# First block's x turned into banks by features, an identity turned in front of it, weights' low parts moved between the first evictions, gate sums in four parts

## The chip, the cores and the metric
One NeuronCore of a Trainium2 chip. The metric is the device time of the whole program in microseconds, the median of several runs.

## The reference
x is 16 x 1024 tokens of 512 features, taken here as 16384 rows. What is computed, in short:

```python
x = x + linear_attn(layernorm(x))   # 16 heads of 32; phi = elu + 1 on q and k, causal sums of k v^T and k
x = x + moe(layernorm(x))           # softmax gate over 8 experts, top 2, capacity 1.25*N/E
# an expert over its capacity (counts > cap) is dropped whole: valid = (counts <= cap)[a_e]
```

Projections are `x @ W.T + b`; the attention output divides the numerator `q . sum(k v^T)` by `q . sum(k) + 1e-6`.

## The kernel before, in words
The 16384 tokens are 32 blocks of 512 (`BT`), each of 4 tiles of 128 (`TPB`). A block passes three stages: **turn** (x normalised, features on the partitions, split into a high part `xt_hi` and a low part `xt_lo` of reduced-precision floats), **proj** (K, Q and V), and **attn** (scores, numerators, output product, residual). In the steady state one step (`Step`) runs attn of one block, proj of the next and turn of the one after it, interleaved by tile `c` = 0 to 3. The program starts with a step that only turns block 0, then a step that projects block 0 and turns block 1 (`attn` is false in both); each engine's `body(st)` is its own list in program order, and `run` calls it. Nothing reorders these lists: an instruction that waits holds all behind it on its engine.

Every product is three products, hi*hi, hi*lo, lo*hi, over 4 groups of features `k`: 12 matmuls of 512 columns make one K or Q chunk (`project`, L660), two times 12 of 260 columns a V chunk (`two_halves`, L678). Below, K0 is chunk 0 of K, and so on; the order on TensorE is K0 Q0 K1 Q1 K2 Q2 K3 Q3 V0 V1 V2 V3. Their results go to a ring of six PSUM banks: K0, K1 to bank 0, Q0, Q1 to bank 1, K2, K3 to bank 5, Q2, Q3 to bank 0. After a K or Q chunk ScalarE does a Relu and an Exp from the bank (`relu_exp`, L848 and L850) and VectorE `phi` (L944) reads the bank and frees it; for K, `key_sums` adds a scan (L954) and a copy (L956). V chunks are evicted by `values` (L963, L965).

The start: SyncE loads x, then the weights (256 KB pieces by 128 columns for K and Q, whole for Wo, Wv, Wo^T). VectorE takes moments (L1016), GpSimd the reciprocal deviations, VectorE normalises (L996). TensorE turns tile c into bank c by four transposes (`turn_first`, L648), ScalarE takes `xt_hi` (L854), VectorE `xt_lo` (L1002). Each weight piece is split the same way: `split_high` on ScalarE (L327), `split_low` on VectorE (L332). Before, ScalarE splits all eight K and Q pieces, and VectorE all eight low parts, in front of the first eviction (`split_first`, `set_first`):

```python
def set_first():
    split_low(dve, "wq_t", 0)
    set_biases(dve)
    for name, g in SPLITS[2:2 * KD]:
        split_low(dve, name, g)
```

Wv is split in one piece in front of K2's eviction. `sum_gates` (L377) multiplies Wo's stage with the gate's 8 columns, 4 products for each of 4 groups: groups 0 and 1 behind Q2, 2 and 3 behind Q3:

```python
if c == 1 and not attn:
    sum_gates(pe, (0, 1))
```

In the second step VectorE also takes `divide` (L992, q times the reciprocal denominator) and the low parts of block 1 (`split_x_low`, L1008) in front of V3's eviction. Block 1's K0 goes to V3's bank 0, so it waits for that eviction.

## Time and profile before

| | |
|---|---|
| median of 3 runs | 1926.53 us (1926.5 to 1927.26) |
| profiled execution, device time | 1929.05 us |
| its span | 1927.3 us |
| granted TensorE clock, mean | 0.996 |
| TensorE busy | 98% |
| VectorE, ScalarE, GpSimd busy | 82%, 34%, 46% |
| DMA | 218 MB, mean 113 GB/s |

Read it so: the span is the profiled execution from its first to its last instruction; the device time has 1.75 us more around it. The profiled execution is 2.5 us above the median of the runs that were only timed.

### The profile page before, as it was taken

The numbers are of one execution on the slowest core, as the hardware profiler recorded it, in microseconds if no ns is written. First come the engines' busy times: TensorE is split into PE (matmuls) and PEld (weight loads), VectorE is DVE, ScalarE is ACT, GpSimd is POOL, SyncE is SP. The second block draws the span as 40 slices with busy tenths as digits, with TensorE's granted clock in tenths as the row PEclk, the third lists the DMA queues.
The fourth block names the chain that finished last, engine by engine and source line by source line (L and its number), as shares of the span: only waits on it lengthen the run. The fifth ranks groups of instructions, "written<-read, shape, count | busy, mean of one in ns | idle before, by whom it ended". The sixth has DMA issues, their size and how long they took to land. (4 is left out here: it accounts for less than half of the span.)

```text
span 1927.3 us, 60211 instructions
## 1 busy us (share of the span) xinstructions
PE 1894.4 (98%) x25412; PEld 1662.2 (86%) x25412; DVE 1580.7 (82%) x3379; ACT 663.7 (34%) x1297; POOL 890.8 (46%) x981
## 2 busy tenths in 40 slices
PE   7999999999999999999999999999999999999996
PEld 6888888888888888888888888888888888888885
DVE  6878777888879887878878987878788897878787
ACT  4333333333333333333333333333333333333331
POOL 3345553455453555534554444555445544355522
PEclk9999999999999999999999999999999999999998
DMA  6343234333233332333433344323433324343222
GB/s 208 100 133 111 87 108 132 117 119 111 91 123 120 124 122 76 123 123 111 128 101 103 112 124 131 111 90 108 130 116 122 106 89 127 120 124 122 73 72 79
DMA packets 171199, 218.00 MB, mean 113 GB/s; under 512 B 24368, under 2 KB 85808, under 8 KB 170928
## 3 DMA queue, kind: packets, MB, share of 16 engines
q1 hardware_dynamic: 170928, 214.13, 35.3%
q8 instruction: 201, 3.29, 0.7%
q14 instruction: 70, 0.57, 0.1%
HBM read 151.02 MB, written 63.04 MB: 111 GB/s over the span
## 5 line engine op out<-in xcount | busy, mean ns | idle before, releaser
L1286 POOL TENSOR_TENSOR k_sum<-k_sum,q_raw 128x512 f32<-128x512 f32 x128 | 165.3, 1291 | 553.0 <-DVE q_raw L944 553.0
L848 ACT ACTIVATE e_tmp<-ring,bias_n 128x512 f32<-128x512 f32 x256 | 176.2, 688 | 508.9 <-PE ring L660 506.5
L933 DVE TENSOR_TENSOR s_mask<-ring,causal 128x512 f32<-128x512 f32 x512 | 314.6, 675 | 0.0
L678 PE MATMUL ring<-wv_hi,xt_hi 128*128 128x260 f32 x1024 | 298.9, 292 | 0.0
L678 PE MATMUL ring<-wv_hi,xt_lo 128*128 128x260 f32 x1024 | 289.2, 282 | 0.0
L678 PE MATMUL ring<-wv_lo,xt_hi 128*128 128x260 f32 x1024 | 289.2, 282 | 0.0
L678 PE MATMUL ring<-wo_hi,o_hi 128*128 128x260 f32 x1024 | 287.0, 281 | 2.0 <-ACT o_hi L898 1.9
L678 PE MATMUL ring<-wo_hi,o_lo 128*128 128x260 f32 x1024 | 286.7, 284 | 1.1 <-DVE o_lo L1185 1.1
L678 PE MATMUL ring<-wo_lo,o_hi 128*128 128x260 f32 x1024 | 287.7, 282 | 0.0
L898 ACT ACTIVATE o_hi<-num_ps 128x512 fp32r<-128x512 f32 x128 | 76.4, 597 | 467.9 <-PE num_ps L758 467.9
L660 PE MATMUL ring<-xt_hi,wk_hi 128*128 128x512 f32 x512 | 208.6, 407 | 3.3 <-DVE xt_lo L1002 1.7
L1281 POOL TENSOR_TENSOR x_in<-x_in,x_rows 128x512 f32<-128x512 f32 x124 | 204.2, 1647 | 9.7
L1279 POOL TENSOR_TENSOR x_in<-x_in,x_rows 128x512 f32<-128x512 f32 x124 | 198.1, 1598 | 18.3 <-DMA x_rows<-moments_rows 18.3
L678 PEld LDWEIGHTS ring<-wv_hi,xt_hi 128*128 128x128 f32 x1024 | 192.7, 188 | 12.1 <-issue 0.4
L660 PE MATMUL ring<-xt_hi,wk_lo 128*128 128x512 f32 x512 | 201.6, 394 | 0.0
L660 PE MATMUL ring<-xt_lo,wk_hi 128*128 128x512 f32 x512 | 200.6, 392 | 0.0
L660 PE MATMUL ring<-xt_hi,wq_lo 128*128 128x512 f32 x512 | 199.6, 390 | 0.0
L660 PE MATMUL ring<-xt_hi,wq_hi 128*128 128x512 f32 x512 | 199.2, 389 | 0.0
L660 PE MATMUL ring<-xt_lo,wq_hi 128*128 128x512 f32 x512 | 199.2, 389 | 0.0
L678 PEld LDWEIGHTS ring<-wo_hi,o_hi 128*128 128x128 f32 x1024 | 192.8, 188 | 5.3 <-ACT o_hi L898 2.4
L944 DVE SCALAR_TENSOR_TENSOR k_t<-ring,bias,e_tmp 128x512 f32<-128x512 f32 x128 | 95.9, 749 | 121.3 <-ACT e_tmp L850 116.7
L678 PEld LDWEIGHTS ring<-wo_lo,o_hi 128*128 128x128 f32 x1024 | 192.1, 188 | 2.9
(142 smaller groups left out, 4055.2 us busy)
## 6 DMA issues: line engine op xcount, KB each, us to landing
x_tok<-in_x SPq DMA_DIRECT2D x128, 256.0 KB, 3.9
res<-in_x SPq DMA_DIRECT2D x128, 256.0 KB, 2.7
out<-res SPq DMA_DIRECT2D x128, 256.0 KB, 2.1
x_in<-in_x_t SPq DMA_DIRECT2D x124, 256.0 KB, 4.6
keys_turned<-k_turned SPq DMA_DIRECT2D x112, 256.0 KB, 2.0
k_tok<-keys_turned SPq DMA_DIRECT2D x448, 64.0 KB, 2.0
x_rows<-moments_rows SPq DMA_DIRECT2D x31, 512.0 KB, 3.6
k_t<-in_wk_t SPq DMA_DIRECT2D x4, 256.0 KB, 4.5
```

Of the source, the lines that this page charges most:

```text
L660: mm = pe.matmul(bank, w[a][:, k, g * P:(g + 1) * P], xt[b][:, k, :], start=n == 0, stop=n == 3 * KD - 1)
L678: mm = pe.matmul(bank[:, 0:HW], rows[a](k), w[b][:, k, h, :], start=n == 0, stop=n == 3 * KD - 1)
L848: act.activation(e_tmp[:, m], bank, ACT.Relu, bias=bias_n[:, m, g:g + 1], scale=-1.0).then_inc(phi_relu.handle, 1)
L898: act.activation(o_wide[0], num, ACT.Copy).then_inc(o_hi.handle, 1)
L933: dve.tensor_tensor(s_mask[:, j], ring[:, st.bank(u)].rearrange("p (g t) -> p g t", g=KD), repeat(causal, KD), ALU.mult).then_inc(free[st. ...
L944: dve.scalar_tensor_tensor(out, bank, bias[:, m, g:g + 1], e_tmp[:, m], ALU.add, ALU.max).then_inc(free[st.bank(u)].handle, 1)
L1279: pool.tensor_tensor(x, x, repeat(x_rows[:, :, c, 0], KD), ALU.subtract).then_inc(x_centred.handle, 1)
L1281: pool.tensor_tensor(x, x, repeat(x_rows[:, :, c, 1], KD), ALU.mult).then_inc(x_normed.handle, 1)
L1286: pool.tensor_tensor(k_sum[:, g], k_sum[:, g], q_raw[:, g], ALU.mult).then_inc(prod.handle, 1)
```

## The change
Parts, in the order of the program:

1. Wk's stage is now `s_mask`, Wq's the second half of `q_div`, so that the stages outlive the first evictions into `k_t` and `q_raw`. Pieces 0 and 1 of both are loaded ahead of the small columns (biases, gate) instead of piece 0 alone.
2. `keep_busy`: 24 transposes of the identity into bank 0, once the second tile's moments are taken.
3. `turn_first` writes the transpose of feature group k to bank 2+k at the tile's columns, so a bank holds one feature group of all four tiles, and is full with the last tile. ScalarE and VectorE split bank by bank; `project_first` does K0 in the order hi*hi, hi*lo(weights), lo*hi for each k, waiting for each k's own parts.
4. ScalarE's and VectorE's splits of the other pieces stand between the first evictions; Wv is split in two halves. The scans follow later. VectorE takes block 1's moments behind Q0's eviction.
5. The gate sums are four parts, behind K2, Q2, K3 and Q3.
6. In the second step VectorE takes the low parts of block 1's tiles 0 and 1 ahead of V2's eviction, instead of behind `divide`; GpSimd's `rstds` come before its first product.

```diff
+TURN_BANKS = [2 + k for k in range(D // P)]
+WARMING = 24
...
-                    load_weights(sp, LOADS[:2])
+                    load_weights(sp, LOADS[:4])
                     load_columns(sp)
-                    load_weights(sp, LOADS[2:-3])
+                    load_weights(sp, LOADS[4:-3])
...
+        def keep_busy():
+
+            pe.wait_ge(x_stat.handle, x_stat.at(2))
+            for _ in range(WARMING):
+                pe.transpose(ring[:, 0, 0:P], ident, ident)
+
         def turn_first(c):
 
-            pe.wait_ge(free[c].handle, free[c].at(0))
             pe.wait_ge(x_normed.handle, x_normed.at(c + 1))
-            for k in range(KD):
-                mm = pe.transpose(ring[:, c, k * P:(k + 1) * P], x_tok[:, c, k * P:(k + 1) * P], ident)
-            mm.then_inc(full[c].handle, 1)
+            for k, b in enumerate(TURN_BANKS):
+                if c == 0:
+                    pe.wait_ge(free[b].handle, free[b].at(0))
+                mm = pe.transpose(ring[:, b, c * P:(c + 1) * P], x_tok[:, c, k * P:(k + 1) * P], ident)
+                if c == TPB - 1:
+                    mm.then_inc(full[b].handle, 1)
+
+        def project_first():
+
+            u = ("K", 0)
+            bank = ring[:, BANK[u]]
+            pe.wait_ge(free[BANK[u]].handle, free[BANK[u]].at(0))
+            pe.wait_ge(ready["wk_t"].handle, 1)
+            for k, b in enumerate(TURN_BANKS):
+                pe.wait_ge(xt_hi.handle, xt_hi.at(k + 1))
+                for a in range(2):
+                    pe.matmul(bank, w_k[a][:, k, 0:P], xt[0][:, k, :], start=k == 0 and a == 0, stop=False)
+                pe.wait_ge(free[b].handle, free[b].at(1))
+                mm = pe.matmul(bank, w_k[0][:, k, 0:P], xt[1][:, k, :], start=False, stop=k == KD - 1)
+            mm.then_inc(full[BANK[u]].handle, 1)
...
-                if c == 1 and not attn:
-                    sum_gates(pe, (0, 1))
...
+                if c == 1 and not attn:
+                    for place in range(2, 4):
+                        chunks(st, c, place)
+                        sum_gates(pe, (place,))
...
+        def first_chunks(st):
+
+            split_high(act, "wk_t", 1)
+            split_high(act, "wq_t", 1)
             act.wait_ge(bias_set.handle, BIASES)
+            relu_exp(st, "K", 0)
+            split_high(act, "wk_t", 2)
+            split_high(act, "wq_t", 2)
+            relu_exp(st, "Q", 0)
+            split_high(act, "wk_t", 3)
+            split_high(act, "wq_t", 3)
+            relu_exp(st, "K", 1)
+            split_high(act, "wv_t", 0)
+            relu_exp(st, "Q", 1)
+            split_high(act, "wv_t", 1)
...
+                if c == 2 and not attn:
+                    split_x_low(st, 0)
+                    split_x_low(st, 1)
```

Where the instructions stand. **ScalarE, evictions of K1 to K2**: `v_tok` is Wv's stage, `e_tmp` what Relu and Exp write. Before:

```order
L848 ACTIVATE e_tmp<-ring,bias_n 128x512 [waits ring_free0,ring_full0]
L850 ACTIVATE e_tmp<-e_tmp 128x512 [waits phi_relu]
L848 ACTIVATE e_tmp<-ring,bias_n 128x512 [waits ring_free1,ring_full1]
L850 ACTIVATE e_tmp<-e_tmp 128x512 [waits phi_relu]
L327 ACTIVATE wv_hi<-v_tok 128x8x256 [waits load_wv_t]
L848 ACTIVATE e_tmp<-ring,bias_n 128x512 [waits ring_free0,ring_full5]
L850 ACTIVATE e_tmp<-e_tmp 128x512 [waits phi_relu]
```

Now:

```order
L877 ACTIVATE e_tmp<-ring,bias_n 128x512 [waits ring_free0,ring_full0]
L879 ACTIVATE e_tmp<-e_tmp 128x512 [waits phi_relu]
L330 ACTIVATE wv_hi<-v_tok 128x4x256 [waits load_wv_t]
L877 ACTIVATE e_tmp<-ring,bias_n 128x512 [waits ring_free1,ring_full1]
L879 ACTIVATE e_tmp<-e_tmp 128x512 [waits phi_relu]
L330 ACTIVATE wv_hi<-v_tok 128x4x256 [waits load_wv_t]
L877 ACTIVATE e_tmp<-ring,bias_n 128x512 [waits ring_free0,ring_full5]
L879 ACTIVATE e_tmp<-e_tmp 128x512 [waits phi_relu]
```

The split of Wv, which waits for its load, stood behind Q1's Relu and Exp; now its first half stands ahead of them.

**VectorE, evictions of K1 to K2**: `k_t` and `q_raw` are what phi writes, `k_sum` the scan. Before:

```order
L944 SCALAR_TENSOR_TENSOR k_t<-ring,bias,e_tmp 128x512 [waits phi_exp,ring_full0]
L954 SCALAR_TENSOR_TENSOR k_sum<-k_t 128x512 [waits ring_free0]
L956 COPY k_carry<-k_sum 128x1 [waits k_scan]
L944 SCALAR_TENSOR_TENSOR q_raw<-ring,bias,e_tmp 128x512 [waits phi_exp,ring_full1]
L332 TENSOR_TENSOR wv_lo<-v_tok,wv_hi 128x8x256 [waits high_split]
L338 CAST wv_hi<-gates 128x8x4
L340 TENSOR_TENSOR wv_lo<-gates,wv_hi 128x8x4 [waits gate_split]
L944 SCALAR_TENSOR_TENSOR k_t<-ring,bias,e_tmp 128x512 [waits phi_exp,ring_full5]
L954 SCALAR_TENSOR_TENSOR k_sum<-k_t 128x512 [waits ring_free5]
```

Now:

```order
L984 SCALAR_TENSOR_TENSOR k_t<-ring,bias,e_tmp 128x512 [waits phi_exp,ring_full0]
L335 TENSOR_TENSOR wk_lo<-s_mask,wk_hi 128x4x128 [waits high_split]
L984 SCALAR_TENSOR_TENSOR q_raw<-ring,bias,e_tmp 128x512 [waits phi_exp,ring_full1]
L335 TENSOR_TENSOR wq_lo<-q_div,wq_hi 128x4x128 [waits high_split]
L994 SCALAR_TENSOR_TENSOR k_sum<-k_t 128x512 [waits ring_free0]
L996 COPY k_carry<-k_sum 128x1 [waits k_scan]
L984 SCALAR_TENSOR_TENSOR k_t<-ring,bias,e_tmp 128x512 [waits phi_exp,ring_full5]
```

Wv's low part left the place in front of K2's phi; Wk's and Wq's last low parts and K0's scan came there.

**TensorE, the start**: `ring` is the PSUM ring. Before:

```order
L648 MATMUL ring<-ident,x_tok 128x128 [waits x_normed,ring_free0,ident_set]
L648 MATMUL ring<-ident,x_tok 128x128 x3
L648 MATMUL ring<-ident,x_tok 128x128 [waits x_normed,ring_free1]
L648 MATMUL ring<-ident,x_tok 128x128 x3
L648 MATMUL ring<-ident,x_tok 128x128 [waits x_normed,ring_free2]
L648 MATMUL ring<-ident,x_tok 128x128 x3
L648 MATMUL ring<-ident,x_tok 128x128 [waits x_normed,ring_free3]
L648 MATMUL ring<-ident,x_tok 128x128 x3
L660 MATMUL ring<-xt_hi,wk_hi 128x512 [waits ring_free3,ready_wk_t,ring_free2,ring_free0,ring_free1]
L660 MATMUL ring<-xt_lo,wk_hi 128x512
```

Now:

```order
L649 MATMUL ring<-ident 128x128 [waits x_stat,ident_set]
L649 MATMUL ring<-ident 128x128 x23
L657 MATMUL ring<-ident,x_tok 128x128 [waits ring_free2,x_normed]
L657 MATMUL ring<-ident,x_tok 128x128 [waits ring_free3]
L657 MATMUL ring<-ident,x_tok 128x128 [waits ring_free4]
L657 MATMUL ring<-ident,x_tok 128x128 [waits ring_free5]
L657 MATMUL ring<-ident,x_tok 128x128 [waits x_normed]
L657 MATMUL ring<-ident,x_tok 128x128 x3
L657 MATMUL ring<-ident,x_tok 128x128 [waits x_normed]
L657 MATMUL ring<-ident,x_tok 128x128 x3
L657 MATMUL ring<-ident,x_tok 128x128 [waits x_normed]
L657 MATMUL ring<-ident,x_tok 128x128 x3
```

The 24 transposes of the identity are new and first; the turning is 16 transposes in both.

## Rows read from the trace of the kernel before

**Rows 1.** Page, busy time of TensorE over the span.
```profile
PE 1894.4 (98%) x25412; PEld 1662.2 (86%) x25412; DVE 1580.7 (82%) x3379; ACT 663.7 (34%) x1297; POOL 890.8 (46%) x981
```

**Rows 2.** Waits of PE over the whole span: us in total, times, longest us.
```profile
PE ring L660 <- DVE gate_x L965: 1.3, 1, 1.3
PE ring L660 <- DVE k_t L944: 0.3, 1, 0.3
```

**Rows 3.** Timeline, PE, first block: start us, us, engine, line, op, [idle before].
```profile
9.79 3.65 PE L648 MATMUL ring<-ident,x_tok 128*128 128x128 f32 x16 [9.79 <-DVE x_tok L996]
...
15.15 0.76 PE L660 MATMUL ring<-xt_hi,wk_hi 128*128 128x512 f32 x1 [1.72 <-DVE xt_lo L1002]
15.71 0.63 PE L660 MATMUL ring<-xt_lo,wk_hi 128*128 128x512 f32 x1
16.14 0.63 PE L660 MATMUL ring<-xt_hi,wk_lo 128*128 128x512 f32 x1
...
19.50 0.40 PE L660 MATMUL ring<-xt_hi,wk_lo 128*128 128x512 f32 x1
```

**Rows 4.** Timeline, DVE and ACT, beside the turning.
```profile
4.53 0.66 DVE L1016 BATCH_NORM_STATS2 stats<-x_tok 128x6 f32<-128x512 f32 x1
...
9.10 1.92 DVE L996 TENSOR_SCALAR x_tok<-x_tok,mv 128x512 f32<-128x512 f32 x4 [0.68 <-POOL mv L1261]
...
13.47 0.60 ACT L854 ACTIVATE xt_hi<-ring 128x512 fp32r<-128x512 f32 x1 [0.26 <-PE ring L648]
...
14.10 0.69 DVE L1002 TENSOR_TENSOR xt_lo<-ring,xt_hi 128x512 fp32r<-128x512 f32 x1 [0.16 <-ACT xt_hi L854]
```

**Rows 5.** Timeline, PE, around the gate sums.
```profile
33.38 1.84 PE L377 MATMUL num_ps<-gates,q_div 128*128 128x8 f32 x16
35.52 0.47 PE L660 MATMUL ring<-xt_hi,wk_hi 128*128 128x512 f32 x1 [0.29 <-DVE k_t L944]
...
39.93 0.39 PE L660 MATMUL ring<-xt_hi,wq_hi 128*128 128x512 f32 x1
...
42.65 1.85 PE L377 MATMUL num_ps<-gates,q_div 128*128 128x8 f32 x16
44.35 0.37 PE L678 MATMUL ring<-wv_hi,xt_hi 128*128 128x260 f32 x1
```

**Rows 6.** Windows, PE: window, us, busy (instructions), PEclk, DMA share, GB/s.
```profile
36.00:37.00 1.00, 1.00 (x4) 0.50 0.49 186
```

**Rows 7.** Timeline, ACT and DVE, around the split of V's weights.
```profile
29.40 1.90 ACT L327 ACTIVATE wv_hi<-v_tok 128x2048 fp32r<-128x2048 f32 x1
31.21 0.67 ACT L848 ACTIVATE e_tmp<-ring,bias_n 128x512 f32<-128x512 f32 x1
31.91 0.63 ACT L850 ACTIVATE e_tmp<-e_tmp 128x512 f32<-128x512 f32 x1
...
31.34 3.05 DVE L332 TENSOR_TENSOR wv_lo<-v_tok,wv_hi 128x2048 fp32r<-128x2048 f32 x1 [0.53 <-ACT wv_hi L327]
...
34.62 0.74 DVE L944 SCALAR_TENSOR_TENSOR k_t<-ring,bias,e_tmp 128x512 f32<-128x512 f32 x1
35.40 1.22 DVE L954 TENSOR_TENSOR_SCAN k_sum<-k_t 128x512 f32<-128x512 f32 x1
```

**Rows 8.** DMA issues (us to landing), SP's timeline, and one window's load.
```profile
v_tok<-in_wv_t SPq DMA_DIRECT2D x1, 1024.0 KB, 11.0
...
18.10 0.51 SPq L311 DMA_DIRECT2D v_tok<-in_wv_t  x1
...
7.50:9.50 2.00, 0.00 (x0) 0.00 (x0) 1.17 (x4) 0.63 (x1) 1.68 (x6) 1.00 0.68 56
```

**Rows 9.** Timeline, DVE, ACT and PE, end of the first projections.
```profile
58.11 2.49 DVE L1008 TENSOR_TENSOR xt_lo<-x_in,xt_hi 128x512 fp32r<-128x512 f32 x4
...
58.79 0.63 ACT L861 ACTIVATE xt_hi<-x_in 128x512 fp32r<-128x512 f32 x1 [2.88 <-PE ring L678]
...
61.15 0.47 PE L660 MATMUL ring<-xt_hi,wk_hi 128*128 128x512 f32 x1 [1.28 <-DVE gate_x L965]
```

More of the change, by code:

```diff
@@ L456, in give @@
             eng.sem_inc(s.handle, s.credit)
-    base_m1 = [int(k < TPB) for k in range(NBANK)]
+    base_m1 = [int(k in TURN_BANKS) for k in range(NBANK)]
     base_0 = [a + b for a, b in zip(base_m1, per_bank(("proj", "turn")))]
@@ L519, in load_x @@
             if a == 1:
-                for c in range(TPB):
-                    sp.wait_ge(full[c].handle, full[c].at(1))
+                for k in TURN_BANKS:
+                    sp.wait_ge(full[k].handle, full[k].at(1))
             if a > 1:
@@ L777, in body @@
             if not attn and not proj:
+                keep_busy()
                 for c in range(TPB):
@@ L782, in body @@
                 last = c == TPB - 1
-                if proj:
-                    if c == 0 and not attn:
-                        for k in range(TPB):
-                            pe.wait_ge(free[k].handle, free[k].at(1))
-                    elif c == 0:
+                if c == 0 and not attn:
+                    project_first()
+                    chunks(st, c, 1)
+                elif c == 1 and not attn:
+                    for place in range(2):
+                        chunks(st, c, place)
+                        sum_gates(pe, (place,))
+                elif proj:
+                    if c == 0:
                         pe.wait_ge(xt_lo.handle, xt_lo.at(TPB * (st.off + 1)))
@@ L814, in body @@
                     scores(st, st.off + 1, 0)
-                if c == 1 and not attn:
-                    sum_gates(pe, (2, 3))
                 if attn:
@@ L878, in body @@
             if not attn and not proj:
-                for c in range(TPB):
-                    split_first_high(c)
+                for k, b in enumerate(TURN_BANKS):
+                    split_first_high(k, b)
                 return
@@ L889, in body @@
                     split_x_high(st, 1)
-                if c == 1 and not attn:
-                    split_high(act, "wv_t")
-                if proj:
+                if c == 0 and not attn:
+                    first_chunks(st)
+                elif proj:
                     chunks(st, c, 0, 1)
@@ L1150, in body @@
                 split_low(dve, "wk_t", 0)
-                for c in range(TPB):
-                    split_first_low(c)
+                set_biases(dve)
+                for k, b in enumerate(TURN_BANKS):
+                    split_first_low(k, b)
                 return
@@ L1155, in body @@
                 last = c == TPB - 1
-                if c == 1 and not attn:
-                    split_low(dve, "wv_t")
-                    split_gates(dve, "wv_t", gw.rearrange("p k (h e) -> p k h e", h=2), 0)
                 if c < 2 and attn and proj:
@@ L1166, in body @@
                     residual_moments(st, 2)
-                if proj:
+                if c < 2 and not attn:
+                    (first_chunks, next_chunks)[c](st)
+                elif proj:
                     chunks(st, c, 0, 1)
@@ L1170, in body @@
                     divide(st)
-                if c == 0 and not attn:
-                    moments(st, range(TPB))
-                if last and turns:
+                if last and attn and turns:
                     split_x_low(st, 0)
@@ L1212, in body @@
                     split_x_low(st, 3)
-                if proj and (attn or c != 2):
+                if proj and (attn or last):
                     chunks(st, c, 2, 3)
@@ L1236, in body, with first_chunks, next_chunks @@
                 last_logits(st)
-        def set_first():
+        def first_chunks(st):
             split_low(dve, "wq_t", 0)
-            set_biases(dve)
-            for name, g in SPLITS[2:2 * KD]:
-                split_low(dve, name, g)
+            split_low(dve, "wk_t", 1)
+            phi(st, "K", 0)
+            split_low(dve, "wq_t", 1)
+            split_low(dve, "wk_t", 2)
+            phi(st, "Q", 0)
+            split_low(dve, "wq_t", 2)
+            moments(st, range(TPB))
+            phi(st, "K", 1)
+            split_low(dve, "wk_t", 3)
+            phi(st, "Q", 1)
+            split_low(dve, "wq_t", 3)
+            key_sums(st, 0)
+        def next_chunks(st):
+            phi(st, "K", 2)
+            key_sums(st, 1)
+            phi(st, "Q", 2)
+            split_low(dve, "wv_t", 0)
+            key_sums(st, 2)
+            split_low(dve, "wv_t", 1)
+            split_gates(dve, "wv_t", gw.rearrange("p k (h e) -> p k h e", h=2), 0)
+            phi(st, "K", 3)
+            key_sums(st, 3)
+            phi(st, "Q", 3)
             set_from_constants(dve)
@@ L1246, in _ @@
         give(dve, *free, o_lo, x1_stat)
-        run(dve, body, set_first)
+        run(dve, body)
         choose(5, range(CHOOSE_STEPS))
@@ L1358, in body @@
                     pool.tensor_tensor(res[:, c % 2], res[:, c % 2], bo_row, ALU.add).then_inc(res_bias.handle, 1)
+                if c == 0 and not attn:
+                    rstds(st)
                 if proj:
                     chunks(st, c, 0, 1)
-                if c == (1 if attn else 0) and turns:
+                if c == 1 and attn and turns:
                     rstds(st)
```

44 lines of the change are left out of this document (21 added, 23 removed).

## The prediction
> **What bounds the kernel now.** I read the page's busy times first: TensorE is busy 98% of the span [rows 1]. So only its gaps and slow stretches are worth looking for, and its list of waits puts those of the projections at 1.3 and 0.3 us, once each [rows 2]; both lie in the first 62 us, the only stretch that the change rewrites. Behind it TensorE is nearly never idle, so what it gains or loses up to block 1's K0 (start 61.15 us) I carry to the end in full.
>
> In the timeline of that stretch three things cost TensorE time. First, a late and slow start: the turning begins at 9.79, the first real matmul at 15.15 after 1.72 us of idle, and these matmuls take 0.63 us each, 0.43 us apart, where later ones take 0.40 [rows 3]. Twelve matmuls of K0 thus last to 19.73 (19.50 plus one pace of 0.23). The pace at the full level is Q3's: 39.93 to 42.65 for 12, 2.72 us or 0.227 each [rows 5]. Second, the gate sums: 16 instructions of 8 columns from 33.38, then 0.29 us idle for VectorE's phi of K2, and K3 starts at 35.52. It needs 4.41 us, until 39.93, instead of 2.72 [rows 5]; the granted clock is 0.50 in that stretch, the lower level of 1.2 GHz [rows 6]. TensorE had done only the narrow gate products and nothing for 2.14 us before the clock fell. The second run of gate sums, 1.70 us, did not bring it down [rows 5]. Third, 1.28 us idle before block 1's K0, for V3's eviction, which stands on VectorE behind the low parts of block 1 [rows 9].
>
> **The change, part by part.**
>
> *Warming and turning.* The transposes of the identity may start when the second moments are done, 5.19 us [rows 4], say 5.3. Sixteen transposes took 3.65 us, some 0.21 each [rows 3]; 24 take 5.1 us, to 10.4, which is 0.6 later than the turning starts now. That is the cost if the clock stays low. At the high level they would take half, and the x tiles (from 9.10, four in 1.92 us [rows 4]) would set the pace instead. Bounds: turning later by 0.6, or its end earlier by 1.6 to 2. I take the first, from the row nearest to it: the present 16 transposes run from 9.79 to 13.44, and 1.7 us later the matmuls still run at the slow pace [rows 3]. So the last four transposes end at 13.4, 13.6, 13.8 and 14.05. The page "TensorE: Matmul & The Clock Gate" of the Trainium skill, section on PE-mode transpose, says that transpose-mode work does not count as busy for the clock gate; by that rule the 24 transposes are pure cost, and the trace does not contradict it.
>
> *K0 piece by piece.* Now K0 waits for the whole chain turn, high part (0.60), low part (0.69), and the hand-over of 0.36 (14.79 to 15.15) [rows 3, 4]. After, its first matmul needs only the high part of bank 2: 13.4 + 0.6 + 0.36 = 14.35. The parts of the next banks follow every 0.6 us (VectorE's and ScalarE's pace in such a row), while the three matmuls of one bank need 1.28, so none of them waits. If the clock rises at the same time as now (about 18.9), 10.7 of the 12 run slow, and K0 is over at 19.2: 0.5 earlier. If it rises 3.8 us after the first matmul, as now, at 18.8.
>
> *Splits between evictions.* On their own they fit: the K and Q pieces that chunk n+1 needs are split while chunk n runs. From K0's end the chunks need 4 x 2.72 for Q0, K1, Q1, K2, then 0.85 of gates, 2.72 for Q2, 0.85: K3 could start at 19.2 + 15.35 = 34.6. But ScalarE's queue now holds the first half of Wv's split ahead of Q1's Relu. Wv's load is issued at 18.10 and lands 11.0 later, at 29.1 [rows 8], where ScalarE would be there at 19.2 + 7 = 26.2. Loading K and Q pieces 1 ahead of the columns fills part of a stretch in which the queues move 56 GB/s [rows 8]; the columns then push pieces 2 and 3 back by 1.1 us, so I take Wv 0.4 earlier, 28.7 (bounds 27.5 and 29.6). From the landing: half split 0.95, Relu and Exp 1.35, phi of Q1 0.75, Wq's last low part 0.65, K0's scan and copy 1.35, phi of K2 0.75, hand-over 0.15: 6.0 us [rows 4, 7]. K3 starts at 34.7, by this chain or by TensorE's own, which meet here. Term: 35.52 - 34.7 = **0.8**. It cannot go below nothing unless Wv lands past 29.5.
>
> *Gate sums in four.* The work is the same, 2 x 1.70 or 4 x 0.85. Each low stretch is 0.85 us between two chunks of 2.72, less than half of the 1.70 that left the clock up [rows 5]. K3 at full pace: 4.41 - 2.72 = **1.7**. Bounds: nothing (if the clock falls for another reason) and 1.7.
>
> *V0 to V2.* VectorE is then busy without a pause from Q1's phi to V0's evictions: phis, scans, two halves of Wv's low part (3.05 in one piece [rows 7]). Counted instruction by instruction it has V0's first bank free in time for V1; this hides within about 0.2 us, and if Wv's low halves take more than 1.5 each it appears one for one. I put it at nothing.
>
> *Low parts before V2's eviction.* VectorE spends 2.49 us on four low parts between divide and V3's eviction [rows 9]. Two go away from there. But the last of them needs its high part, and ScalarE waits for V3's end on TensorE with that (58.79, 0.63 long [rows 9]). So V3's eviction moves from 60.52 to about 60.05 in these times, not by 1.25: **0.45**.
>
> Sum: 0.8 + 1.7 + 0.45 = 2.95, rounded to 2.9. The profiled execution would go from 1929.05 to 1926.1 (span 1924.4), and the median, which lies 2.5 below the profiled time, from 1926.53 to **1923.6**. A measurement of this kernel can tell about 0.2%, 3.9 us, from no change: the forecast is a gain that lies within that.
>
> **The rivals.**
>
> *A. The clock's fall at the gate sums is the profiled run's own.* The profiled execution is 2.5 us above the median, and 1.7 of it may be this. For: the second gate stretch left the clock up, so the fall is not certain each time. Against: the timed runs lie within 0.8 us, less than 1.7. Then the gain is 0.8 + 0.45 = 1.25: 1925.3. Chance 0.2.
>
> *B. The warming works.* The identity's transposes raise the clock; K0 runs at the full pace right behind the pieces, ends near 15.5 instead of 19.7. But Wv still holds Q1's Relu until 28.7 + 0.95, so K3 still starts at 34.7; TensorE, done with its work at 15.5 + 15.35 = 30.9, idles 3.8 us, and its clock falls there as after the 2.14 us of now. The early 3.7 us are lost, and the 1.7 perhaps too: 1923.6 to 1925.3. Chance 0.12. For: ScalarE's wait for Wv depends only on its order and the load. Against: the present transposes raised nothing.
>
> *C. Wv comes early and the start is quick.* With the load at 27.3 or before and the warm start, K3 starts at 33.3: 2.2 + 1.7 + 0.45 = 4.35, 1922.2. Chance 0.13, since only both together give it.
>
> *D. Wv comes late, and the new wait costs more than the old.* The last bank now fills at 14.05, so block 1's loads, ahead of Wv in the queue, are issued 0.6 later, and the queue could run dry or the column loads hold the rest up. Up to a landing at 31 the change still breaks even (K3 at 37, no slow stretch). Landing at 32.1, K3 starts at 38.1, TensorE idles 3.5 and K3 is slow again: V0 at 38.1 + 7.15 + 1.7 = 46.95 against 44.35 [rows 5], less 0.45, is 2.1 us slower: 1928.6. Against: 11.0 us to landing shows a deep backlog, which 0.6 us don't empty. Chance 0.05, and 0.03 for over 3.9 us.
>
> **How the numbers follow.** The forecast has 0.5, A 0.2, B 0.12, C 0.13, D 0.05. Faster by over 0.2% means below 1922.7: C and the low tail of the forecast, 0.18. Slower by over 0.2%, 0.03. Within, 0.79. The range runs from 1922.0 (C) to 1926.0 (A with Wv late by 0.7), and leaves out D and the tails, some 0.2.
>
> **What would show it.** In the profile after: first real matmul near 14.35 and at the slow spacing of 0.43; the 24 transposes 0.21 apart, not 0.11; ScalarE idle about 2.4 us at Wv's high part, on the load; K3 at 34.7, 2.7 us long, clock 1.00 from the rise near 19 on; block 1's K0 near 58.2 instead of 61.15, with some 0.8 us of idle before it. A warm K0 makes B or C true; K3 late with a full clock lays it on Wv. If block 1's K0 gains 3 and the time doesn't, the carrying in full is wrong.

## The result, and the profile after

| | before | after |
|---|---|---|
| median | 1926.6 us (1925.62 to 1927.26, 6 runs) | 1935.3 us (1932.71 to 1935.64, 6 runs) |
| ratio | | 1.0038, 95% interval 1.0028 to 1.0049 |
| profiled execution, its span | 1929.05, 1927.3 us | 1932.71, 1930.9 us |
| block 1's K0 starts | 61.15 us [rows 9] | 67.76 us |
| last instruction of VectorE starts | 1921.45 us | 1928.14 us |

The change makes the kernel slower by 0.38%: 8.7 us between the medians, 7.3 by the ratio, where I had forecast 2.9 us less. In the profiles the work ends 6.7 us later (last instruction of VectorE), but the span grows by 3.6 only, because the stretch behind that instruction is 3 us shorter (last section). TensorE is as busy as before, and its list of waits names three new ones. Page and waits of PE, kernel after:

```profile
PE 1900.1 (98%) x25436; PEld 1666.5 (86%) x25436; DVE 1594.3 (83%) x3380; ACT 663.6 (34%) x1298; POOL 894.2 (46%) x981
```
```profile
PE ring L684 <- DVE k_t L984: 3.8, 1, 3.8
PE ring L702 <- DVE gate_x L1005: 2.6, 1, 2.6
...
PE ring L702 <- DVE wv_lo L343: 1.7, 1, 1.7
```

All of it is in the first 68 us. Timeline of PE, kernel after (start us, us, engine, line, op, [idle before]), first block and start:

```profile
5.21 4.39 PE L649 MATMUL ring<-ident 128*128 128x128 f32 x24 [5.21 <-DVE stats L1055]
9.69 2.02 PE L657 MATMUL ring<-ident,x_tok 128*128 128x128 f32 x16
12.16 0.47 PE L670 MATMUL ring<-xt_hi,wk_hi 128*128 128x512 f32 x1 [0.45 <-ACT xt_hi L883]
...
15.21 0.48 PE L684 MATMUL ring<-xt_hi,wq_hi 128*128 128x512 f32 x1
```

The start is far better than forecast. The 24 transposes are 0.18 apart on average: three in each quarter of a microsecond up to 8.5, four or five from there on. The 16 of the turning take 2.02 us [rows 3: 3.65], the first real matmul comes at 12.16, and these matmuls run 0.23 apart from the fourth on (the first three, which wait for their pieces, 0.31 to 0.34). Q0 starts at 15.21; before, at 19.73. Four and a half microseconds are won here. Then, from the gate sums to block 1's K0:

```profile
26.84 1.03 PE L380 MATMUL num_ps<-gates,q_div 128*128 128x8 f32 x8 [0.44 <-DMA q_div<-in_wo]
...
30.56 0.95 PE L380 MATMUL num_ps<-gates,q_div 128*128 128x8 f32 x8
35.34 0.47 PE L684 MATMUL ring<-xt_hi,wk_hi 128*128 128x512 f32 x1 [3.83 <-DVE k_t L984]
...
43.41 0.95 PE L380 MATMUL num_ps<-gates,q_div 128*128 128x8 f32 x8
46.03 0.58 PE L702 MATMUL ring<-wv_hi,xt_hi 128*128 128x260 f32 x1 [1.67 <-DVE wv_lo L343]
...
61.50 0.39 PE L702 MATMUL ring<-wv_hi,xt_hi 128*128 128x260 f32 x1 [2.61 <-DVE gate_x L1005]
...
67.76 0.47 PE L684 MATMUL ring<-xt_hi,wk_hi 128*128 128x512 f32 x1 [0.51 <-DVE gate_x L1005]
```

TensorE idles 3.83 us before K3, which starts at 35.34, as late as before [rows 5: 35.52]; 1.67 us before V0; 2.61 us before V3. And the granted clock falls to its lower level, 1.2 GHz, at each of the three; below, the stretch of matmuls at that level is called slow. Windows of PE (window, us, busy, PEclk, DMA share, GB/s):

```profile
36.00:37.00 1.00, 1.00 (x4) 0.50 0.55 207
46.00:47.00 1.00, 0.97 (x4) 0.51 0.00 0
63.00:64.00 1.00, 1.00 (x7) 0.54 0.00 0
```

K3 is thus as slow as before (4.42 us, to 39.76; before 4.41), V0 takes 4.49 and V3 4.25, where a V chunk of 24 matmuls at the full clock takes 2.96. (The PEclk of this view helps at these three places only. Before a program's first rise it reads 1.00 as well, in the kernel before too, where K0's matmuls are 0.43 apart; there the spacing of the instructions tells the level.) That adds up: V0's wait 1.67 and slow stretch 1.53, V3's wait 2.61 and slow stretch 1.29, the third and fourth gate sums with Q3 between them 0.2 more than Q3 and one double one, less 0.18 at K3's start and 0.77 at K0's wait (1.28 to 0.51): 6.3 of the 6.6 us by which block 1's K0 is late; the scores (L755) behind V3, still slow, take 0.33 more. From there on the shift stays between 6.6 and 7.8 us; the last instruction of VectorE is 6.7 late.

The terms of this sum depend on one another. In e3 below, whose lists behind the start are the same, V0 waits 1.85 us and then runs at the full clock; it ends 1.46 earlier, and still V3 starts at 61.50, now behind 3.17 us of idle. What V0's slow stretch costs, V3's wait gives back.

What TensorE waits for at K3 comes through ScalarE. Timeline of ACT, kernel after:

```profile
29.43 1.06 ACT L330 ACTIVATE wv_hi<-v_tok 128x1024 fp32r<-128x1024 f32 x1 [7.11 <-DMA v_tok<-in_wv_t]
30.40 0.67 ACT L877 ACTIVATE e_tmp<-ring,bias_n 128x512 f32<-128x512 f32 x1
```

Wv lands at 29.4 (issued 18.27, 11.1 us to landing), ScalarE has been idle for 7.11 us, and Q1's Relu stands behind the first half. Q1, finished on TensorE at 23.5, is evicted at 31.8 by VectorE.

What it waits for at V0 and V3 is VectorE, and there the durations changed. V0 waits for its own weights, the low part of the gate columns (L343), and V3 for the eviction of V2. Timelines of DVE and POOL, kernel after:

```profile
33.10 1.22 DVE L994 TENSOR_TENSOR_SCAN k_sum<-k_t 128x512 f32<-128x512 f32 x1
...
35.11 1.84 DVE L994 TENSOR_TENSOR_SCAN k_sum<-k_t 128x512 f32<-128x512 f32 x1
...
37.73 1.85 DVE L335 TENSOR_TENSOR wv_lo<-v_tok,wv_hi 128x1024 fp32r<-128x1024 f32 x1
39.50 2.58 DVE L994 TENSOR_TENSOR_SCAN k_sum<-k_t 128x512 f32<-128x512 f32 x1
...
42.19 2.40 DVE L335 TENSOR_TENSOR wv_lo<-v_tok,wv_hi 128x1024 fp32r<-128x1024 f32 x1
44.51 1.24 DVE L341 CAST wv_hi<-gates 128x32 fp32r<-128x32 f32 x1
...
56.02 1.03 DVE L1239 SCALAR_TENSOR_TENSOR rden<-rden_high,lo_rows,den 128x256 fp32r<-128x256 f32 x1
56.97 4.07 DVE L1047 TENSOR_TENSOR xt_lo<-x_in,xt_hi 128x512 fp32r<-128x512 f32 x2
```
```profile
37.22 1.28 POOL L1349 TENSOR_TENSOR k_sum<-k_sum,q_raw 128x512 f32<-128x512 f32 x1 [1.35 <-DVE k_carry L996]
38.45 2.55 POOL L1342 TENSOR_TENSOR x_in<-x_in,x_rows 128x512 f32<-128x512 f32 x1
41.08 2.42 POOL L1344 TENSOR_TENSOR x_in<-x_in,x_rows 128x512 f32<-128x512 f32 x1
43.47 2.24 POOL L1349 TENSOR_TENSOR k_sum<-k_sum,q_raw 128x512 f32<-128x512 f32 x1
...
56.71 1.86 POOL L1342 TENSOR_TENSOR x_in<-x_in,x_rows 128x512 f32<-128x512 f32 x1
58.65 1.85 POOL L1344 TENSOR_TENSOR x_in<-x_in,x_rows 128x512 f32<-128x512 f32 x1
```

The kernel before, for comparison (DVE and POOL; L332 at 63.71 is Wo's low part, as large as Wv's):

```profile
34.31 0.17 DVE L338 CAST wv_hi<-gates 128x32 fp32r<-128x32 f32 x1
...
63.71 2.28 DVE L332 TENSOR_TENSOR wo_lo<-k_t,wo_hi 128x2048 fp32r<-128x2048 f32 x1
```
```profile
36.69 1.53 POOL L1279 TENSOR_TENSOR x_in<-x_in,x_rows 128x512 f32<-128x512 f32 x1 [4.45 <-DMA x_rows<-moments_rows]
38.30 1.54 POOL L1281 TENSOR_TENSOR x_in<-x_in,x_rows 128x512 f32<-128x512 f32 x1
```

The same scan takes 1.22 us at 33.10 and 2.58 at 39.50; half of Wv's low part 1.85 and 2.40, where I had put at most 1.5; the conversion of the 32 gate columns (L341) 1.24 instead of the 0.17 that it took before; two low parts of x 4.07, where four took 2.49 [rows 9]. Compare the ends: the scan from 39.50 is over at 42.08, and its own 1.2 us would begin at 40.86, near the end of GpSimd's product of 38.45 (41.00). The half from 42.19 is over at 44.59, 1.1 us behind the end of the product of 41.08 (43.50). The conversion ends at 45.75, with the product of 43.47 (45.71). GpSimd's products are stretched as well, 2.55 and 2.42 against 1.53 and 1.54 us for the same two in the kernel before. The two engines take turns. Between K2's phi and V0 five instructions of VectorE are longer by this (0.62, 0.63, 1.36, 1.18 and 1.07), together 4.9 us; without them V0's weights would be ready at about 41.1, three microseconds before TensorE comes to V0 (an estimate from these rows). In the kernel before they hardly met up to block 1's K0; the 3.05 of Wv's low part [rows 7], which runs beside a GpSimd product of 30.95 to 32.24, is the one large trace of it, and Wo's, of the same size, takes 2.28.

The Trainium skill has this, in "SBUF — State Buffer", "Who interferes with whom": a VectorE instruction with two inputs in SBUF contends with a GpSimd instruction that reads SBUF, and the ports that they share are an exclusive lock. The trace agrees: 2.58 instead of 1.22 for a scan.

### The profile page after: what moved, and what is told of

Read it like the earlier page. It is cut to its first block and busy times, and to the rows that moved or that the text cites. A ratio compares the mean times of both kernels' runs of the same rounds, so it can differ in the third digit from the quotient of the medians.

```text
span 1930.9 us, 60259 instructions
## 1 busy us (share of the span) xinstructions
PE 1900.1 (98%) x25436; PEld 1666.5 (86%) x25436; DVE 1594.3 (83%) x3380; ACT 663.6 (34%) x1298; POOL 894.2 (46%) x981
## 5 line engine op out<-in xcount | busy, mean ns | idle before, releaser
L702 PEld LDWEIGHTS ring<-wv_hi,xt_lo 128*128 128x128 f32 x1024 | 194.5, 190 | 0.0
```

The lines of the kernel that those rows point to most:

```text
L702: mm = pe.matmul(bank[:, 0:HW], rows[a](k), w[b][:, k, h, :], start=n == 0, stop=n == 3 * KD - 1)
```

## The experiments

Three theories. **T1**: Wv's wait ahead of Q1's Relu idles TensorE and lets the clock fall; everything that is late there then falls together on VectorE. **T2**: the low parts ahead of V2's eviction hold V3. **T3**: VectorE's instructions are late because GpSimd's products block them. Rivals: the identity, the turning or the gate sums in four cost the time. Ratios are to the kernel before on the same chip.

**e1: Wv's halves behind K2's and Q2's Relu and Exp on ScalarE** (VectorE's order stays).

```diff
-                elif proj:
+                elif proj and (attn or c != 1):
                     chunks(st, c, 0, 1)
...
             relu_exp(st, "K", 1)
-            split_high(act, "wv_t", 0)
             relu_exp(st, "Q", 1)
+            relu_exp(st, "K", 2)
+            split_high(act, "wv_t", 0)
+            relu_exp(st, "Q", 2)
             split_high(act, "wv_t", 1)
```

> Only ScalarE's order changes: the two halves of Wv's high part stand behind K2's and Q2's Relu and Exp instead of in front of Q1's and K2's. Theory 1 (ScalarE holds Q1's Relu until Wv lands near 29.4, and TensorE waits 3.8 us at K3 for that): the wait at K3 goes, K3 starts at 31 to 32 instead of 35.34 and at the full clock (2.7 us instead of 4.4); VectorE's Wv low halves are done before GpSimd begins with block 1 near 37, so V0 starts at 37.8 to 40 instead of 46.03. Block 1's K0 comes 5 us or more earlier than 67.76, and the time falls by 5 to 9. Rival (VectorE is short of time in this stretch whatever ScalarE does): K3 starts earlier, but V0 stays within 2 us of 46 and the time within 2 us.

Measured: 1928.98 us (1926.84 to 1934.56, 10 runs), ratio 1.0007 [0.9997, 1.0017]. K3 starts at 32.47 and runs at the full clock, V0 at 39.81 without a wait, block 1's K0 at 63.27 instead of 67.76. V3 still waits 3.12 us and is slow. Timelines of PE and DVE, e1:

```profile
55.76 0.58 PE L702 MATMUL ring<-wv_hi,xt_hi 128*128 128x260 f32 x1 [3.12 <-DVE gate_x L1007]
...
63.27 0.47 PE L684 MATMUL ring<-xt_hi,wk_hi 128*128 128x512 f32 x1 [0.64 <-DVE gate_x L1007]
```
```profile
51.28 4.02 DVE L1049 TENSOR_TENSOR xt_lo<-x_in,xt_hi 128x512 fp32r<-128x512 f32 x2
```

T1's share is 4.5 us of the start of block 1's K0; T2's is left.

**e2: the low parts of tiles 0 and 1 back behind `divide`.**

```diff
-                if c == 2 and not attn:
-                    split_x_low(st, 0)
-                    split_x_low(st, 1)
...
-                if last and attn and turns:
+                if last and turns:
                     split_x_low(st, 0)
                     split_x_low(st, 1)
```

> Only VectorE's low parts of block 1's tiles 0 and 1 go back behind divide. Theory 1 (these two, 4.07 us for 2, wait behind GpSimd's normalisation of the last tile and hold V2's eviction, so V3 waits 2.6 us and runs at the low clock): V3's wait of 2.61 us goes, V3 takes 3.1 instead of 4.3, block 1's K0 comes 3 to 3.5 us earlier than 67.76, K3 stays at 35.3. Rival (the two just take long in this place for a reason of their own, such as memory traffic, and do so anywhere): four low parts behind divide take over 4 us, and block 1's K0 gains less than 1 us.

Measured: 1931.76 us (1929.12 to 1937.07, 10 runs), ratio 1.0022 [1.0013, 1.0032]. V3 starts at 57.97 without a wait, K0 at 63.50 with one of 1.29, as before the change; K3 is as late as after (35.08, behind 3.71 us of idle), and slow (5.26 us). Block 1's K0 is 4.3 us earlier than after; 0.85 of it is there when V1 starts (51.58 and 52.43), ahead of the edit, because V0 waits less here (0.64) and keeps the full clock. From V1's start to block 1's K0 it is 15.33 us after, 11.92 in e2 and 11.93 before. So T2's share is 3.4 us: the 0.45 us that the move was to bring were in truth a loss of over seven times as much.

**e3: no transposes of the identity** (`keep_busy()` taken out).

> The 24 transposes of the identity are left out, nothing else. If they raised the clock (the records of the changed kernel show it granted from 8.5 us on): K0's matmuls come 0.43 us apart again, Q0 starts at 18 to 19.5 instead of 15.2, and as K3 waits for the chain from Wv's landing anyway, K3 stays at 35.3 and block 1's K0 within 0.5 us of 67.76. If the clock rose for another reason: K0 stays fast without them. If the early start is worth something at the end: the time gets 2 us or more longer.

Measured: 1935.05 us (1934.37 to 1937.22, 4 runs), ratio 1.0043 [1.0027, 1.0060]. The 16 transposes from 9.78 take 3.65 us as before, Q0 starts at 16.80, K3 at 35.41, K0 at 68.10. So the identity is worth 1.6 us at Q0 in this pair (0.5 and 0.7 in the pairs e5 and e8, e9 and e10), nothing at K3, and is not what makes the kernel slow. I had expected Q0 at 18 or later; the clock rises at 14.5 even so, four microseconds earlier than before, though the turning begins at the same time: K0 by pieces follows the turning 0.13 us behind it, where it used to idle 1.72 [rows 3].

**e4: the gate sums in two parts again** (behind Q2 and Q3).

> The gate sums stand in two parts again, behind Q2 and behind Q3; the rest is the changed kernel. Theory 1: the clock falls at K3 because TensorE idles 3.8 us there, not because of the sums, so K3 is slow in both, the starts of K3 and V0 stay within 0.5 us (35.3 and 46.0), and the time stays. Rival (four parts lower TensorE's activity in more places): the clock's falls change in number and the time by 1 us or more.

Measured: 1934.79 us (1933.61 to 1935.84, 5 runs), ratio 1.0038 [1.0024, 1.0052]. K3 at 35.65 behind 3.76 us of idle, slow; block 1's K0 at 68.58, where e11, the change once more, has 68.57. No difference from the change: with 3.8 us of idle before K3 its clock fell with the sums in two parts as with four.

**e5: e1 and e2 together.**

> Both edits of the first two runs in one: Wv's halves behind K2's and Q2's Relu and Exp, the low parts back behind divide. Theory 1 (the two losses are separate, one for ScalarE's wait, one for VectorE behind GpSimd): K3 near 32.5, V0 near 39.8, V3 without a wait and near 52.6, block 1's K0 at 57.8 to 58.5, which is 9 to 10 us earlier than the changed kernel and 3 earlier than the kernel before; the time 2.5 to 3.5 us below the kernel before. Rival (the low parts only move their wait behind GpSimd to another place): block 1's K0 no earlier than 61, the time that of the kernel before.

Measured: 1925.42 us (1921.08 to 1928.25, 8 runs), ratio 0.9977 [0.9966, 0.9989]. Block 1's K0 at 60.17, some 2 us later than expected. One of the three waits is left, V0's, 1.65 us at 41.38, and a slow stretch behind it: VectorE's last half of Wv's low part takes 2.44 at 36.21, and the two instructions on the gate columns 1.52 and 1.20, beside GpSimd's products from 35.60 to 41.28.

**e6: GpSimd normalises one column of 128 in each tile of block 1** (block 1 stays almost wholly unnormalised; all else as after).

```diff
-            x = x_in[:, :, c * P:(c + 1) * P]
+            w = P if st.has("attn") else 1
+            x = x_in[:, :, c * P:c * P + w]
```

> The changed kernel, with GpSimd's normalisation of block 1 cut to one of 128 columns of each tile, so block 1 is left mostly unnormalised; ScalarE and VectorE do the same work. Theory 1 (VectorE instructions with two operands in SBUF wait for the end of a GpSimd instruction that runs): the scans beside it take 1.2 instead of 1.8 and 2.6, Wv's second low half 1.2 instead of 2.4, the two low parts 1.3 instead of 4.1; V0's wait of 1.67 and V3's of 2.61 go; K3 stays at 35.3; block 1's K0 comes at 60 to 63. Rival (memory traffic or TensorE's reads slow them): they take as long as now and block 1's K0 stays near 67.8.

Measured: 1927.07 us (1925.59 to 1928.14, 8 runs), ratio 0.9993 [0.9983, 1.0003]. VectorE's list is word for word that of the change. Timelines of DVE and POOL, e6:

```profile
34.86 1.83 DVE L994 TENSOR_TENSOR_SCAN k_sum<-k_t 128x512 f32<-128x512 f32 x1
...
37.46 1.85 DVE L335 TENSOR_TENSOR wv_lo<-v_tok,wv_hi 128x1024 fp32r<-128x1024 f32 x1
39.23 1.21 DVE L994 TENSOR_TENSOR_SCAN k_sum<-k_t 128x512 f32<-128x512 f32 x1
...
40.55 1.22 DVE L335 TENSOR_TENSOR wv_lo<-v_tok,wv_hi 128x1024 fp32r<-128x1024 f32 x1
41.68 1.27 DVE L341 CAST wv_hi<-gates 128x32 fp32r<-128x32 f32 x1
...
53.45 1.29 DVE L1047 TENSOR_TENSOR xt_lo<-x_in,xt_hi 128x512 fp32r<-128x512 f32 x2
```
```profile
38.19 1.18 POOL L1343 TENSOR_TENSOR x_in<-x_in,x_rows 128x4 f32<-128x4 f32 x1
...
40.72 2.20 POOL L1350 TENSOR_TENSOR k_sum<-k_sum,q_raw 128x512 f32<-128x512 f32 x1 [0.27 <-DVE k_carry L996]
```

The scan that took 2.58 takes 1.21, the half 1.22 for 2.40, the two low parts 1.29 for 4.07. What still stands beside a product over 512 columns (the 1.83, 1.85 and 1.27) is as long as before. K3 is as late as ever (35.09), but V0 and V3 wait no more, and block 1's K0 starts at 60.95, 6.8 us earlier than after. T3 is shown: nothing changed but GpSimd's work, and VectorE's durations followed. It also shows that T2's instructions are cheap in themselves.

**e7: the kernel before, with only the gate sums in four.**

> The kernel before with only the gate sums in four parts. Theory 1 (the sums in two parts brought the clock down at K3): K3 starts at 35.5 as before, takes 2.7 instead of 4.4, V0 starts 1.7 earlier (42.7), the time falls by 1.7 where the clock fell in every run of the kernel before, by less where it fell in some. Rival (the idle before K3 or chance brings it down): K3 is slow again in this profile, or the time is the same within 0.5 us.

Measured: 1927.19 us (1926.73 to 1928.79, 11 runs), ratio 0.9996 [0.9987, 1.0005]. K3 starts at 35.15 behind 0.21 us of idle and takes 2.8 us; V0 at 42.46, K0 at 59.25, both 1.9 earlier than before, and the span is 1925.4 against 1927.3. Of the 1.9, 0.4 is there at Q0 already (19.34 against 19.73), which the edit does not touch; from K3's start to V0's it is 7.31 us against 8.83. So the term of 1.7 measured 1.5 in the trace. The timed runs give less, 0.8 us with an interval that reaches nothing; that the fall of the clock in the profiled run is not in every run (my rival A) would explain the difference, but was not tried by itself.

The start of this run, where the code is that of before, shows one thing more. Timeline of PE, e7:

```profile
9.82 3.24 PE L648 MATMUL ring<-ident,x_tok 128*128 128x128 f32 x16 [9.82 <-DVE x_tok L1000]
14.93 0.47 PE L660 MATMUL ring<-xt_hi,wk_hi 128*128 128x512 f32 x1 [1.87 <-DVE xt_lo L1006]
```

The turning takes 3.24 us instead of 3.65, and the first five matmuls of K0 are 0.30, 0.24, 0.23 and 0.23 us apart; from there to Q0 they are 0.43 apart. Here the 16 transposes of x raised the clock by themselves, at about 12.5, and it fell again behind the 1.87 us of idle.

**e8: e5 without the identity.**

> As the run with both edits, and without the 24 transposes of the identity. If the early clock is worth something once the Wv wait is gone: K0 ends later by 0 to 3 us (by when the clock rises), K3 and all behind it later by as much, time up to 3 us above the run with both edits. If K3 is still bound by the chain from Wv's landing: K3 within 0.5 us of it and the time the same.

Measured: 1926.99 us (1925.42 to 1928.16, 11 runs), ratio 0.9990 [0.9981, 0.9999]. The program ran differently from what e5 would lead one to think: Q0 starts 0.5 us later than in e5 (17.21), but V0 at 39.97 with no wait, and K0 at 58.15, two microseconds earlier than e5's. GpSimd's products fell between other instructions of VectorE: the first on block 1 begins at 36.99, behind a load (`x_rows`), and in e5 at 35.60. Who meets whom is a matter of tenths, and moving VectorE's gate columns out of the way was to settle it.

**e9: e5, with the gate columns' conversion and low part (L341, L343) ahead of K0's scan**, so that nothing small stands between Wv's second half and V0.

```diff
             split_low(dve, "wq_t", 3)
+            split_gates(dve, "wv_t", gw.rearrange("p k (h e) -> p k h e", h=2), 0)
             key_sums(st, 0)
...
             split_low(dve, "wv_t", 1)
-            split_gates(dve, "wv_t", gw.rearrange("p k (h e) -> p k h e", h=2), 0)
```

> The run with both edits, and the two small VectorE instructions that split the gate's columns of Wv's tile moved ahead of K0's scan, as they need no load that comes late. Theory 1 (in the run with both edits V0 waited 1.65 us for the second of them, which stood behind GpSimd's normalisation, and ran at the low clock): V0 follows Q3 at once (38.8 to 40.0), block 1's K0 at 57.3 to 58.5, the time 0.5 to 3 below the run with both edits and 3 to 5 below the kernel before. Rival (the last Wv low half or K2's scan waits there instead): V0 still waits 1 us or more.

Measured: 1923.61 us (1921.93 to 1925.81, 9 runs), ratio 0.9976 [0.9966, 0.9986]. It is 0.24% faster than the kernel before, and 0.5% faster than the change, which e11 repeats on the same chip (1934.05). Its block 1's K0 is the earliest but for e10's; its time cannot be told from that of e5 (0.9977), where I had expected 0.5 to 3 us less. Timeline of PE, e9:

```profile
39.48 0.37 PE L702 MATMUL ring<-wv_hi,xt_hi 128*128 128x260 f32 x1
...
51.60 0.39 PE L702 MATMUL ring<-wv_hi,xt_hi 128*128 128x260 f32 x1
...
57.13 0.47 PE L684 MATMUL ring<-xt_hi,wk_hi 128*128 128x512 f32 x1 [1.29 <-DVE gate_x L1007]
```

VectorE takes the two halves of Wv's low part in 1.21 and 1.22 us (33.65 and 36.10), the second over 0.4 us after GpSimd's first product on block 1 begins at 36.93. V0 follows the gate sums at once, V3 needs no wait, K0 starts at 57.13, four microseconds before [rows 9], and the clock stays at 1.00 from 10.3 until 1908. That the edit is what took V0's wait away is not shown: GpSimd begins 1.3 us later than in e5, and in e8, which has e5's order and the same late begin, V0 did not wait either.

**e10: e9 without the identity.**

> The same without the 24 transposes of the identity. K0's end is 0 to 3 us later by when the clock rises, and since no wait stands between K0 and V0 any more, block 1's K0 is later by the same. On the two profiles so far that was 0.5 us (16.74 and 17.21): the time is the same within 1 us, if the clock rises near 15; 2 us more, if it rises near 19.

Measured: 1925.78 us (1924.25 to 1926.85, 11 runs), ratio 0.9985 [0.9976, 0.9994]. K0 starts at 57.01, no later than in e9, though Q0 is 0.7 us later; VectorE ends earlier (1918.58 against 1919.77), and still the span is longer, 1924.1 against 1922.6. I had expected the same time within 1 us. From VectorE's last instruction to the end of the span it is 5.5 us here and 2.8 in e9.

**e11: the change once more**, beside e9 and e10 on their chip.

> The changed kernel once more, on the chip of the next two, so that the three stand beside one another. If the loss is what its trace shows, block 1's K0 comes 6 to 8 us later than in the kernel before (61.15) in this profile too, V3's wait and K3's wait of over 2.5 and 3.5 us are there, and the time is 6 to 9 us above the kernel before. If the earlier trace was an outlier, one of these waits is missing or under 1 us.

Measured: 1934.05 us (1933.27 to 1936.44, 8 runs), ratio 1.0029 [1.0018, 1.0039]. K0 at 68.57 (67.76 in the first profile): the same three waits, 3.83, 1.95 and 3.12 us. So profiles of one kernel differ by 0.8 us at this place, and differences below that between the runs above carry nothing. Q0 starts at 16.41 here, 1.2 later than in the first profile. And the clock does not fall at V0, which takes 2.97 us behind its wait of 1.95; it falls at K3 and V3.

**e12: the kernel before, with only the 24 transposes of the identity.**

```diff
+            if c == 0:
+                pe.wait_ge(x_stat.handle, x_stat.at(2))
+                for _ in range(24):
+                    pe.transpose(ring[:, 0, 0:P], ident, ident)
             pe.wait_ge(free[c].handle, free[c].at(0))
```

> The kernel before with nothing added but the 24 transposes of the identity in front of the turning, behind the second tile's moments. Two questions. First, do they raise the clock by themselves: then K0's matmuls run 0.23 apart from their first one on (before: 0.43 up to about 18.9) and Q0 starts near 17.5 instead of 19.73; if other edits of the change raised it, Q0 stays at 19.7 or later. Second, what that start is worth: K3 is held by Wv's load (landed 29.1) through ScalarE's queue, so K3 stays at about 35.5 behind a longer idle time, V0 near 44.4, and block 1's K0 stays within 0.5 us of 61.15. Theory (the end of the program, not its start, is what the identity is worth): from the last instruction of VectorE to the end of the span it takes 2.8 us instead of the 5.8 of before, and the time is 2 to 3 us below that of before, ratio about 0.999. Rival (the end has nothing to do with the identity): the stretch stays at 5 to 6 us and the ratio is 1.000 to 1.001.

Measured: 1926.48 us (1923.10 to 1931.31, 11 runs), ratio 0.9991 [0.9982, 1.0000]. Timeline of PE, e12:

```profile
5.49 4.88 PE L648 MATMUL ring<-ident 128*128 128x128 f32 x24 [5.49 <-DVE stats L1020]
10.21 1.91 PE L652 MATMUL ring<-ident,x_tok 128*128 128x128 f32 x16
14.40 0.47 PE L664 MATMUL ring<-xt_hi,wk_hi 128*128 128x512 f32 x1 [2.28 <-DVE xt_lo L1006]
14.71 0.39 PE L664 MATMUL ring<-xt_lo,wk_hi 128*128 128x512 f32 x1
...
34.89 0.77 PE L664 MATMUL ring<-xt_hi,wk_hi 128*128 128x512 f32 x1 [1.87 <-DVE k_t L948]
```

The transposes raise the clock by themselves: the turning takes 1.91 us [rows 3: 3.65] and K0 runs 0.23 apart from its second matmul on, though TensorE was idle for 2.28 us before it. Nothing comes of it at K3: 1.87 us of idle, the slow stretch longer (5.25 us), block 1's K0 at 61.56 against 61.15. The end does change. VectorE's last instruction starts at 1926.76 and the span ends at 1929.5, 2.8 us later, where before it was 5.8 (1921.45 to 1927.3). That this execution was late by then by 5.3 us has other places: it is 0.4 at block 1's K0, 2.6 at the last scan, and the rest comes in the last block. Its timed runs lie 1.9 us below those of before, in an interval that just touches no change.

## Why the prediction was wrong, point by point

**Right.** The bound: TensorE was to be read by its gaps and slow stretches, and block 1's K0 carried its shift to the last matmul (+6.6 there, +6.7 at the end). In the timed runs the step from there to the time is looser: +8.7 on the first chip, +5.6 (0.29%) in e11. The carrying is not in full in every profile either: from block 1's K0 to VectorE's last instruction, against before, +7.4 became +10.4 in e11, -4.0 became -1.7 in e9, +0.4 became +5.3 in e12. The gate sums in four give K3 1.5 of its 1.7 us when nothing else interferes (e7). ScalarE does wait for Wv's load ahead of Q1's Relu.

**"The first, from the row nearest to it": the warming costs 0.6 and the clock stays low.** Wrong. The clock is at its upper level from 8.5 on, during the identity's transposes, and e12 shows that they alone do it. The rule of the Trainium skill ("TensorE: Matmul & The Clock Gate", section on PE-mode transpose, that such work doesn't count as busy) spoke against it; the measurement decides otherwise. The row that I took, the turning's, is one execution's: in e7 the same 16 transposes did raise the clock, before they were over. That the present transposes "raised nothing" was read from one profile.

**"From the landing ... 6.0 us. K3 starts at 34.7."** The chain was right, and measured it took 5.9 us. The landing was not: 29.4 instead of 28.7, later than the 29.1 of before; Wv is issued at 18.27 instead of 18.10, so nothing was gained by the pieces that now go ahead of the columns. The term of 0.8 was 0.2. (TensorE's own chain of 15.35 adds up to 15.30, which changes nothing.) The larger error is that the forecast let this chain meet TensorE's own at 34.7: with the quick start TensorE is there at 31.5, so the 3.8 us of idle of rival B came true, and with them the fall of the clock. **K3 at full pace, 1.7**, was therefore nothing. Rival B named the mechanism, the 3.8 us and the fall, but priced all that followed as in the forecast; it had a chance of 0.12, and no case had more than 0.03 of being clearly slower.

**"I put it at nothing": V0 to V2.** This is the first of the two steps that turned the sign. V0's wait of 1.67 us and the slow stretch of 1.53 are 3.2 us in this profile; in e11 it is the wait alone, 1.95. I counted VectorE's list with durations of the kernel before, in which GpSimd stood still beside them, and asked only whether the sum fitted and V0's bank was free for V1. What held TensorE was V0 itself, whose weights VectorE finishes with L343. The warning was on record in my own sentence, that Wv's low halves above 1.5 us would appear one for one: they were 1.85 and 2.40, and a scan went from 1.22 to 2.58.

**"0.45": the low parts ahead of V2's eviction.** The second. I priced what goes away behind `divide`, not the new place: between V2's reciprocal denominators and its eviction, two low parts cost 4.07 us beside GpSimd's normalisation of block 1's last tile, V3 waited 2.61 us and ran slow for 1.29 more. From V1's start on, e2 gives 3.4 us for this edit. In block 1's K0 e2 is 4.3 us earlier than after, e1, for Wv's place, 4.5, and both together (e5) 7.6; that is 1.2 short of the sum, and V0's wait of 1.65 us has come back in e5. e6 shows that under V0's wait and V3's lies the same cause, since it takes both away, and 6.8 us with them, without touching either edit. It leaves K3's wait as it is: that one is Wv's load on ScalarE (e1), and against the kernel before it costs nothing but the start that was won.

**Rivals.** A stays open (e7); the profile of e12 has the slow K3 too, behind 1.87 us of idle. C's 33.3 for K3 was reached and passed once Wv stood behind K2: 32.1 to 32.5 in e1, e5 and e9. D's mechanism, a late Wv, came with a delay of 0.3 and not of 3. None of them had VectorE and GpSimd in it, and that was the missing one. The range, built from the bounds of terms that all shared the unstalled durations, could not hold the outcome.

## What to carry to other kernels

When an edit moves VectorE work with two SBUF operands, look in the timeline at what GpSimd does at the new place, and price each such instruction at its own duration plus what is left of the GpSimd product; the list that fitted by its sum was late by 4.9 us here. A load that an engine's queue waits for belongs behind every eviction that feeds the next chunk: here its place in ScalarE's queue was worth 4.5 us, and a start made 4.5 us quicker was worth nothing until it had been moved. After each idle stretch of TensorE read the granted clock: in the first profile the change's three waits, 8.1 us together, were followed by stretches at 1.2 GHz that cost 4.5 us more, in e11 only two of the three. And one profile shows only one course of the clock: the start of e7, with the code of the kernel before, ran at another level than the start of before.

## What the runs showed of the hardware

- **VectorE and GpSimd take turns where VectorE's operands are in SBUF.** A scan of 128x512 took 1.22, 1.84 and 2.58 us by what GpSimd did beside it; two low parts 1.29 and 4.07; GpSimd's product 1.53 and 2.55. It holds for instructions of a few columns too: a conversion of 128x32 with one input took 0.17 and 1.24, `lo_rows`, of one column, 0.16 and 1.06. It does not hold for all: `divide`, with one operand in PSUM, takes 2.48 us for four beside a GpSimd product (e8, from 52.71, product from 53.03) and 2.47 without one (after, from 61.77).
- **Transposes raise the clock.** With the 24 transposes of the identity from 5.2 to 5.8 on, the nine profiles have the upper level from 8.5 to 11.7. The 16 transposes of x alone, from 9.8 on, brought it at 12.5 (e7) and 12.8 (e10), before any real matmul; with matmuls close behind it came at 14.5 and 15.3 (e3, e8), and in the kernel before at 18.9.
- **Two microseconds of idle do not settle whether the clock falls.** It fell around waits of 1.63 (e4, V3), 1.65 (e5, V0), 1.67 (after, V0), 1.87 (e7 at K0, e12 at K3) and 1.91 us (e4, V0), and stayed up over 1.85 (e3, V0), 1.95 (e11, V0) and 2.28 us (e12, K0). It fell around all of 2.6 us and more.
- **The end of the program depends on code at its start.** In the five profiles of kernels without the identity (before, e3, e7, e8, e10) the span ends 5.1 to 6.0 us after VectorE's last instruction starts; in the nine with it, 2.8. The trace's record of TensorE's last branch, over code that it skips, takes 2.9 to 4.0 us in the first and 0.4 to 0.5 in the second. Four pairs have it in the timed runs, by ratios to before: e5 and e8 0.9977 and 0.9990, e9 and e10 0.9976 and 0.9985, e12 and before 0.9991 and 1, the change and e3 1.0038 and 1.0043. All four point the same way, but in no pair are the two intervals clear of each other. So what the identity is worth here, 1 to 2.5 us, comes at the end, not at the start that it was added for: block 1's K0 is no earlier with it in e9, e5 and e12. Part of the 3 us is lost on the way. From the scans of block 2 to the last one, the profiles with the identity lose 0.3 to 2.6 us against before, in steps of up to 0.9, those without it change by -0.5 to +0.3; why was not looked into. Why 24 more instructions ahead make the branch short was not tried: that it is where the code behind them comes to lie is only a guess.
